# Attention plus top-2 expert layer on one core: second expert matmul in split float16, experts ordered by block count, weights converted piece by piece during the blocks, weight norms on TensorE

## The chip, the cores and the metric

The kernel runs on one core of a Trainium2 chip. The metric is device time in microseconds (us) of one execution. A core has TensorE (PE; its weight loads are listed as PEld), VectorE (DVE), ScalarE (ACT), GpSimd (POOL) and SyncE (SP), which here only issues transfers. Each has its own instruction stream; they meet at semaphores. In the profile an engine's name with a q (DVEq) is its instruction sequencer, which loads registers, waits for semaphores and hands work to the engine proper.

## What is computed

Input x is 16 tiles of 128 tokens with 256 features. First a channel attention with a residual, then an expert layer with a residual:

```
x   = x + xattn(layernorm(x), ctx, ctx)          # 4 heads, attention over channels, two weight sets
xf  = layernorm(x)                               # 2048 tokens x 256
logits = xf @ gate_w                             # 8 experts
top_w, top_idx = top_k(logits, 2);  combine = softmax(top_w) scattered
h   = gelu(xf @ w1[e] + b1[e])                   # 256 -> 1024
y   = h @ w2[e] + b2[e]                          # 1024 -> 256
out = x + sum_e combine[t, e] * y[e]
```

## The kernel before

**Attention stage.** 16 tiles pass through a software pipeline of 24 iterations (`attention(i, u)`, one function per engine, i from -4 to 19; iterations 4 to 9 are a loop, the rest is unrolled). In iteration i, PE forms the channel scores of tile i+1 (L913), transposes the context of tile i+2 (L921), transposes the normed output of tile i-3 (L929), multiplies with the values for tile i-1 (L937), forms the router logits of tile i-4 (L948), and last transposes the probabilities of tile i (L956), which wait for DVE (L726). DVE normalizes and scales (L660, L670, L713, L726) and adds the residual (L734, tile i-1). POOL makes k (L473, L476) and the inverse deviations (L461, L464).

**First-layer weights.** w1 (8 MB) lands in the storage of `W2`. ACT squares it (L570) in iterations 4 to 11, a ones-matmul sums the squares (L902), POOL takes the power -0.5 (L486), and each expert is scaled and split into a float16 high and low part in `W1`. Six experts are split inside iterations 13 to 19 by ACT (L575, L580), DVE (L697, L702) and POOL (L491); the last two after the stage, by ACT (L600, L604) and POOL (L500). Only when an expert is split can w2 of that expert be loaded over it (L375, L381).

**Routing.** DVE picks the two best experts of each token (L783 to L794, twelve small dependent operations), PE counts ranks, DVE gives each expert's tokens slots padded to blocks of 128 (L799 to L822), builds one-hot tables (L827, eight times), and the table of experts per block (L845 to L850). PE turns the one-hots into a list of rows per slot (L973), which becomes `row_of` (L854).

**Blocks.** There are NB = 39 blocks of 128 token slots, in order of the expert's number. `experts(i, u)` is one iteration on each engine:

```
PE:   transpose rows of block i+1 (L985); first layer of block i, 48 float16 matmuls (L999:
      high*high, high*low, low*high); second layer of block i-1, 8 float32 matmuls of 256 columns
      that the profile shows as 16 records (L1010); bias from three bfloat16 parts (L1012)
ACT:  high part of the rows of block i+1 (L622); Gelu of block i in two halves (L628)
DVE:  low part of block i+1 (L865); read the expert's number of block i+1 (L868) and take its
      routing weight (L870); read the number of block i (L873); hidden = psum*scale + b1 of
      block i in two halves (L877); output of block i-1 times routing weight (L887)
POOL: gather rows of block i+2 (L520, L526); scatter-add block i-2 to DRAM (L532, L537)
SP:   copy the split first-layer weights of block b into XW, two buffers (L393)
```

The hidden activations hT and the second-layer weights are float32. The order on every engine is as written. The sequencer of an engine stops at a semaphore wait, and every `value_load` is a TENSOR_LOAD and register work on it. After the last block the sums are read back and written out (L407, L637).

## Time and profile before

| | |
|---|---|
| median of 3 runs (lowest, highest) | 463.03 us (462.89, 463.79) |
| span of the profiled execution, first to last instruction | 460.8 us |
| the profiled execution's own time | not listed apart; the runs are 2.1 to 3.0 us above its span |
| busy: PE, DVE, ACT, POOL | 360.7, 238.7, 159.8, 234.3 us |
| attention and conversions / routing / blocks / write-back | 0 to 139 / 139 to 171 / 171 to 439 / 439 to 461 us |

A group row reads: line, engine, operation, output<-input by the program's names, shapes, count; then busy time and mean of one in ns; then the idle time of the engine just before, and what ended it. A row of the timeline reads: start in us, us, engine, line, operation, and in brackets the idle time before it and who ended it. A line of the chain reads: start, us, what the execution waited for. Profiled starts are from the start of the span.

### The profile page before, as it was taken

How to read it: one execution, taken by the hardware profiler on the slowest of the kernel's cores; microseconds unless marked ns; L12 is line 12 of the kernel's file. 1: busy time of each engine (PE TensorE's matmuls, PEld its weight loads, DVE VectorE, ACT ScalarE, POOL GpSimd, SP SyncE). 2: the span in 40 equal slices, each digit the busy share in tenths (PEclk: the TensorE clock that was granted, in tenths of full speed). 3: DMA queues.
4: the chain of work that ended last, by engine and by line, in shares of the span. 5: the costliest groups of instructions: out<-in, count | busy, mean ns of one | idle time of the engine just before them, and what ended most of it. 6: DMA issues, size and time to landing. Idle time of an engine off the chain costs nothing.

```text
span 460.8 us, 10869 instructions
## 1 busy us (share of the span) xinstructions
PE 360.7 (78%) x3229; PEld 315.9 (69%) x3230; DVE 238.7 (52%) x457; ACT 159.8 (35%) x399; POOL 234.3 (51%) x286
## 2 busy tenths in 40 slices
PE   0366778898630139999999999999999999999910
PEld 0356777797530028888988988888898898888800
DVE  1899988999899943433433333343343333334200
ACT  1335888867657003122212212222221221222100
POOL 6778777796879223434444543544444454352220
PEclk9999555555555558999999999999999999999965
DMA  7897665521279546566567557556656755764148
GB/s 132 254 317 216 183 175 146 161 69 45 65 243 346 158 155 230 165 225 197 155 220 219 157 195 228 174 171 226 202 153 215 222 158 191 228 181 153 22 84 303
DMA packets 55430, 84.54 MB, mean 183 GB/s; under 512 B 22578, under 2 KB 46996, under 8 KB 50420
## 3 DMA queue, kind: packets, MB, share of 16 engines
q1 hardware_dynamic: 43444, 71.24, 43.5%
q0 software_dynamic: 7680, 10.91, 14.9%
q10 hardware_dynamic: 4288, 2.18, 1.5%
q8 instruction: 8, 0.13, 0.1%
q14 instruction: 10, 0.08, 0.1%
HBM read 31.67 MB, written 11.74 MB: 94 GB/s over the span
## 4 chain that ended last, share of the span: by engine, by line
PE 56%; DMA 1%; issue 1%; POOLq 0%; POOL 0%; DVE 0%; DVEq 0%; ACT 0%
PE bank L1010 29%; PE bank L999 22%; PE bank L985 3%; PE bank L1012 2%; DMA shared<-xn_rows,gix 1%; POOLq L71 0%; POOL acc_rows L537 0%; DVEq L868 0%; DVE shared L887 0%; DVE shared L865 0%; ACT shared L622 0%; POOL six L532 0%; DVE w_of L870 0%; POOLq L536 0%; POOLq L537 0%
## 5 line engine op out<-in xcount | busy, mean ns | idle before, releaser
L1010 PE MATMUL bank<-W,shared 128*128 x624 | 143.3, 383 | 0.0
L1010 PEld LDWEIGHTS bank<-W,shared 128*128 128x128 f32 x624 | 115.5, 190 | 14.2
L999 PE MATMUL bank<-shared,X 128*128 128x128 f16 x1872 | 112.1, 220 | 0.5 <-issue 0.5
L537 POOL DMA_INDIRECT acc_rows<-shared,six x39 | 62.6, 1604 | 98.0 <-DVE shared L887 87.6
L999 PEld LDWEIGHTS bank<-shared,X 128*128 128x128 f16 x1872 | 108.9, 99 | 1.3 <-issue 0.7
L628 ACT ACTIVATE shared<-shared 128x512 f32<-128x512 f32 x78 | 49.1, 630 | 114.4 <-DVE shared L877 113.3
L887 DVE TENSOR_SCALAR shared<-bank,w_of 128x256 f32<-128x256 f32 x39 | 18.9, 484 | 106.7 <-PE bank L1012 106.7
L877 DVE SCALAR_TENSOR_TENSOR shared<-bank,h_unscale,b1T 128x512 f32<-128x512 f32 x78 | 55.3, 747 | 34.5 <-PE bank L999 20.8
L526 POOL DMA_INDIRECT shared<-xn_rows,gix x39 | 39.5, 1012 | 38.7 <-POOL gix L520 29.8
L622 ACT ACTIVATE shared<-bank 128x256 f16<-128x256 f32 x39 | 15.0, 384 | 102.3 <-PE bank L985 102.3
L520 POOL COPY gix<-row_of 128x1 int32 (+1 forms) x39 | 26.6, 683 | 7.4 <-DVE row_of L854 7.4
L937 PEld LDWEIGHTS bank<-shared 128*128 128x128 f32 x128 | 28.5, 326 | 1.8 <-ACT shared L557 1.8
L937 PE MATMUL bank<-shared 128*128 128x64 f32 x128 | 28.5, 402 | 1.0 <-ACT shared L557 0.9
L473 POOL TENSOR_TENSOR shared<-CX,shared 128x512 f32<-128x512 f32 x16 | 23.7, 1481 | 7.1 <-DMA CX<-in_ctx 7.1
L592 ACT ACTIVATE shared<-bank,vcols 128x128 f32<-128x128 f32 x64 | 24.1, 462 | 4.1 <-PE bank L937 3.5
L956 PE MATMUL bank<-ident,shared 128*128 128x128 f32 x32 | 10.5, 428 | 18.6 <-DVE shared L726 18.6
L865 DVE SCALAR_TENSOR_TENSOR shared<-bank,shared 128x256 f16<-128x256 f32 x39 | 16.6, 425 | 14.5 <-ACT shared L622 14.4
L476 POOL TENSOR_TENSOR shared<-shared 128x512 f32<-128x512 f32 x16 | 22.6, 1415 | 1.3
L563 ACT ACTIVATE shared<-bank,nmax 128x64 f32<-128x64 f32 x64 | 19.3, 318 | 11.0 <-DVE nmax L647 11.0
L985 PE MATMUL bank<-ident,shared 128*128 128x128 f32 x78 | 17.6, 308 | 6.5 <-DMA shared<-xn_rows,gix 6.5
L913 PEld LDWEIGHTS bank<-shared 128*64 128x64 f32 x256 | 14.4, 212 | 10.4 <-issue 10.4
L913 PE MATMUL bank<-shared 128*64 128x64 f32 x256 | 17.3, 311 | 5.5 <-POOL shared L476 4.0
(136 smaller groups left out, 426.7 us busy)
## 6 DMA issues: line engine op xcount, KB each, us to landing
X<-W SPq DMA_DIRECT2D x39, 1024.0 KB, 5.0
W<-in_L_ffn_w SPq DMA_DIRECT2D x16, 512.0 KB, 4.3
W<-in_L_ffn_w SPq DMA_DIRECT2D x8, 1024.0 KB, 6.6
CX<-in_ctx SPq DMA_DIRECT2D x32, 128.0 KB, 2.9
X<-in_x SPq DMA_DIRECT2D x4, 512.0 KB, 5.5
acc_rows<-X SPq DMA_DIRECT2D x16, 128.0 KB, 2.3
xn_rows<-xn SPq DMA_DIRECT2D x16, 128.0 KB, 2.2
X<-acc_rows SPq DMA_DIRECT2D x8, 256.0 KB, 5.2
```

The lines of the kernel that those rows point to most:

```text
L473: pool.tensor_tensor(k[:, n].rearrange("p g (h e) -> p g h e", e=HD), c, KW.rearrange("p g (h e) -> p g h e", e=HD), ALU.mult).then_inc(km ...
L520: pool.tensor_copy(gix[:, n:n + 1], row_of[:, bass.ds(b, 1)]).then_inc(gix_ok, 1)
L526: pool.indirect_dma_start(out=XG[:, n, :], out_offset=None, in_=xn_dram, in_offset=bass.IndirectOffsetOnAxis(ap=gix[:, n:n + 1], axis=0))\
L537: pool.indirect_dma_start(out=acc_dram, out_offset=bass.IndirectOffsetOnAxis(ap=six[:, n:n + 1], axis=0), in_=Y[:, n, :], in_offset=None, ...
L592: act.activation(vT[:, n, h, :], pCT[n][:, h, :], ACT.Identity, bias=vcols[:, NH + h:NH + h + 1], scale=vcols[:, h:h + 1]).then_inc(vt_ok, 1)
L628: act.activation(hT[:, n, 4 * m:4 * m + 4, :], hb[:, 4 * m:4 * m + 4, :], ACT.Gelu)\
L877: dve.scalar_tensor_tensor(out=hb[:, 4 * m:4 * m + 4, :], in0=pHT[n][m], scalar=h_unscale[:, bass.ds(e, 1)], in1=b1T[:, bass.ds(e * FC + 4 ...
L913: mm = pe.matmul(pS[n][h * HD:(h + 1) * HD, c, g, :], q[:, n, g, ch], k[:, n, g, ch], start=True, stop=True)
L937: mm = pe.matmul(pO[:, h * HD:(h + 1) * HD], vT[:, n, h, :], aT[:, h // 2, (h % 2) * HD:(h % 2 + 1) * HD], start=True, stop=True)
L985: mm = pe.transpose(pGT[:, c, :], XG[:, n, c * P:(c + 1) * P], ident[:, :])
L999: mm = pe.matmul(pHT[n][m][:, f % 4, :], XW[:, n, c, w, f * P:(f + 1) * P], XT[:, n, x, c, :], start=(c == 0 and w == 0 and x == 0), stop= ...
L1010: pe.matmul(pY[n], hT[:, n, f, :], W2[:, bass.ds(e, 1), f, :].rearrange("p a d -> p (a d)"), start=(f == 0), stop=False)
```

## The change

1. **Second layer in split float16.** w2 is scaled and split into high and low like w1, and so is the hidden activation. The 8 float32 matmuls of a block become 24 float16 matmuls of 256 columns. ACT writes Gelu to `hf` (float32) and then, after its own result, the scaled high part `hT[.., 0]`; DVE writes the low part `hT[.., 1]`. The unscaling goes into the routing weight and b2.
2. **Weights stay where they land** (`W`, nine slots) and are converted in 32 pieces of 1024 columns, one per block: the high part on ACT, the low part on DVE. Each converted expert goes to the slot of the expert before it, the first to a spare slot. Pieces 0 to 3 are made before and in iteration -1; iteration i of the block loop makes piece i+4, for i from 0 to 27. Iterations 28 to 40 convert nothing.
3. **Experts are ordered by block count**, most first, so that the expert of rank r cannot begin before block 4r. DVE computes ranks, the permutation and two tables per block (expert, slot).
4. **Weight norms on TensorE.** All 16 weight halves (w1, w2 of 8 experts, 1 MB each) are loaded during the attention stage, one per iteration from -4. In iterations 1 to 16 PE multiplies each half's top 16 bits, read as bfloat16, with itself: 16 matmuls of 128 columns into one bank. DVE takes the diagonals every fourth iteration (`traces`). ACT's squares and all conversions of the attention stage and behind it are gone.
5. The context transposes have one bank in place of two and come after the logits; b1 is transposed ahead of the attention stage on PE and ACT; b2's three small transfers are issued by ACT after its iteration 2; all 24 attention iterations are unrolled; blocks loop by four. SP does not copy first-layer weights for blocks 0 to 3; PE reads them in the spare slot.

```diff
@@ PE, end of an attention iteration (new)
+                w = i - GRAM
+                if 0 <= w < 2 * E:
+                    pe.wait_ge(w_in[w % 4], 16 * (w // 4 + 1))
+                    after(pe, trace_ok, w // 4)
+                    for j in range(2 * PIECE // P):
+                        x = (w // E) * 2 * PIECE + j * P
+                        cols = Wtop[:, w % E, x:x + P, 1:2].rearrange("p x o -> p (x o)")
+                        mm = pe.matmul(pGram[:, w % 4, :], cols, cols, start=(j == 0), stop=(j == 2 * PIECE // P - 1))
+                    mm.then_inc(gram_ok, 1)
@@ DVE
+            def traces(r):
+                dve.wait_ge(gram_ok, 4 * (r + 1))
+                dve.tensor_tensor(gsq, pGram, ident[:, :].rearrange("p (o f) -> p o f", o=1).broadcast_to([P, 4, P]),
+                                  ALU.mult).then_inc(diag_ok, 1)
+                dve.wait_ge(diag_ok, r + 1)
+                dve.tensor_reduce(wsq[:, 4 * r:4 * r + 4], gsq, AX.X, ALU.add).then_inc(trace_ok, 1)
...
@@ conversions taken out of ACT's and DVE's attention and of POOL's (the late ones also)
-                        act.activation(squares, W1in[:, bass.ds(e, 1), c, :].rearrange("p a f -> p (a f)"), ACT.Square,
-                                       accum_out=w1sq[:, bass.ds(e, 1), c]).then_inc(sq_ok, 1)
...
-                    act.activation(W1[:, e, 0, 0, :], W1in[:, e, 0, :], ACT.Copy, scale=w1scale[:, e:e + 1])\
-                       .then_inc(high_ok[0], 1)
...
-                    dve.scalar_tensor_tensor(out=W1[:, e, 0, 1, :], in0=W1in[:, e, 0, :], scalar=w1scale[:, e:e + 1],
-                                             in1=W1[:, e, 0, 0, :], op0=ALU.mult, op1=ALU.subtract).then_inc(low_ok[0], 1)
...
-                    pool.tensor_tensor(W1[:, e, c, 1, :], W1in[:, e, c, :], W1[:, e, c, 0, :], ALU.subtract)\
-                        .then_inc(low_late, 1)
@@ ACT, block iteration i
+                if not isinstance(i, int) or 0 <= i < CONVERTED - 4:
+                    if u == 0:
+                        held["dst"] = act.value_load(perm[0:1, bass.ds(g + 1, 1)], min_val=0, max_val=E)
+                        held["src"] = act.value_load(perm[0:1, bass.ds(g + 2, 1)], min_val=0, max_val=E - 1)
+                    act.wait_ge(low_ok, i + 1)
+                    high(u, bass.ds(held["src"], 1), bass.ds(held["dst"], 1), wscale[:, u // 2, bass.ds(held["src"], 1)])
                     for m in range(2):
                         act.wait_ge(hb_ok, 2 * b + (m + 1))
-                        act.activation(hT[:, n, 4 * m:4 * m + 4, :], hb[:, 4 * m:4 * m + 4, :], ACT.Gelu)\
-                           .then_inc(gelu_ok, 1)
+                        after(act, lo_ok, 2 * b + (m - 1))
+                        act.activation(hf[:, part, :], hb[:, part, :], ACT.Gelu).then_inc(gelu_ok, 1)
+                        act.wait_ge(gelu_ok, 2 * b + (m + 1))
+                        act.activation(hT[:, n, 0, part, :], hf[:, part, :], ACT.Copy, scale=hscale[:, bass.ds(e, 1)])\
+                           .then_inc(hi_ok, 1)
@@ DVE, iteration -1 of the blocks
+                if isinstance(i, int) and i == -1:
+                    for k in range(2, 4):
+                        dve.wait_ge(high_ok, k + 1)
+                        low(k, first, spare_slot, wscale[:, 1, first])
+                    dve.tensor_tensor(y_scale[:, :], wscale[:, 1, :], hscale[:, :], ALU.mult).then_inc(b2_scaled, 1)
...
+                    dve.tensor_tensor(B2[:, :, :], B2[:, :, :], y_scale[0:3, :].rearrange("r (e o) -> r e o", o=1)
+                                      .broadcast_to([3, E, D]), ALU.mult).then_inc(b2_scaled, 1)
@@ DVE, block iteration i
+                if converting and u == 0:
+                    held["dst"] = dve.value_load(perm[0:1, bass.ds(g + 1, 1)], min_val=0, max_val=E)
+                    held["src"] = dve.value_load(perm[0:1, bass.ds(g + 2, 1)], min_val=0, max_val=E - 1)
                     for m in range(2):
                         dve.wait_ge(h_ok, 2 * b + (m + 1))
+                        dve.scalar_tensor_tensor(out=hb[:, part, :], in0=pHT[n][m],
                                                  scalar=h_unscale[:, bass.ds(e, 1)],
...
+                        if m == 0 and converting:
+                            dve.wait_ge(high_ok, i + 5)
+                            low(u, bass.ds(held["src"], 1), bass.ds(held["dst"], 1),
+                                wscale[:, u // 2, bass.ds(held["src"], 1)])
+                    for m in range(2):
+                        dve.wait_ge(hi_ok, 2 * b + (m + 1))
+                        dve.scalar_tensor_tensor(out=hT[:, n, 1, part, :], in0=hf[:, part, :],
+                                                 scalar=hscale[:, bass.ds(e, 1)], in1=hT[:, n, 0, part, :],
+                                                 op0=ALU.mult, op1=ALU.subtract).then_inc(lo_ok, 1)
@@ PE, second layer of block b = i-1
-                    pe.wait_ge(gelu_ok, 2 * (b + 1))
                     for f in range(FC):
-                        pe.matmul(pY[n], hT[:, n, f, :], W2[:, bass.ds(e, 1), f, :].rearrange("p a d -> p (a d)"),
-                                  start=(f == 0), stop=False)
+                        if f % 4 == 0:
+                            pe.wait_ge(lo_ok, 2 * b + (f // 4 + 1))
+                        for w, h in ((0, 0), (0, 1), (1, 0)):
+                            x = (2 * (2 + f // 4) + w) * PIECE + (f % 4) * D
+                            pe.matmul(pY[n], hT[:, n, h, f, :], whole(Wh[:, slot, x:x + D]),
+                                      start=(f == 0 and w == 0 and h == 0), stop=False)
```

**DVE in the blocks.** One iteration of the loop. Before, from the read of the expert's number (expert) to the output (w_of is the routing weight):

```order
L873 TENSOR_LOAD expert
L873 ISA x2
L875 REGISTER_ALU
L32 REGISTER_ALU [waits h_ok]
L877 ISA [waits gelu_ok]
L877 SCALAR_TENSOR_TENSOR shared<-bank,h_unscale,b1T 128x512
L875 REGISTER_ALU
L877 ISA [waits gelu_ok,h_ok]
L877 SCALAR_TENSOR_TENSOR shared<-bank,h_unscale,b1T 128x512
L32 REGISTER_ALU [waits y_ok]
L887 REGISTER_ALU [waits got_w,added]
L887 TENSOR_SCALAR shared<-bank,w_of 128x256
```

With the change, in the same place, from the first half of the hidden layer to the second low part (L926 is a weight piece's low part, L980 the activation's):

```order
L968 SCALAR_TENSOR_TENSOR shared<-bank,h_unscale,b1T 128x512
L974 REGISTER_ALU
L926 ISA [waits high_ok]
L926 ISA
L926 SCALAR_TENSOR_TENSOR W<-W,wscale 128x1024
L966 REGISTER_ALU
L968 ISA [waits gelu_ok,h_ok]
L968 SCALAR_TENSOR_TENSOR shared<-bank,h_unscale,b1T 128x512
L980 REGISTER_ALU [waits hi_ok]
L980 SCALAR_TENSOR_TENSOR shared<-shared,hscale 128x512
L980 SCALAR_TENSOR_TENSOR shared<-shared,hscale 128x512 [waits hi_ok]
```

A piece of 1024 columns stands between the two halves, and two operations that wait for ACT stand ahead of the output, where there were none.

**PE in the attention stage.** One iteration before (the context transposes are L921, the probabilities' transposes L956):

```order
L913 MATMUL bank<-shared 64x64 [waits exp_ok,k_ok,q_ok]
L913 MATMUL bank<-shared 64x64 x7
L921 MATMUL bank<-ident,CX 128x128 [waits vt_ok,c_in1]
L921 MATMUL bank<-ident,CX 128x128 x3
L929 MATMUL bank<-ident,xn 128x128 [waits xn_ok]
L929 MATMUL bank<-ident,xn 128x128
L937 MATMUL bank<-shared 128x64 [waits x1_ok,vt_ok,as_ok]
L937 MATMUL bank<-shared 128x64 x3
L956 MATMUL bank<-ident,shared 128x128 [waits as_ok,pr_ok]
L956 MATMUL bank<-ident,shared 128x128
```

With the change, the second half of one iteration and the start of the next (L1028 values, L1038 logits, L1046 context, L1054 probabilities, L1066 a weight half with itself, L1012 scores):

```order
L1028 MATMUL bank<-shared 128x64 [waits x1_ok,vt_ok,as_ok]
L1028 MATMUL bank<-shared 128x64 x3
L1038 MATMUL bank<-GW,W 128x8 [waits xts_ok]
L1038 MATMUL bank<-GW,W 128x8
L1046 MATMUL bank<-ident,W 128x128 [waits vt_ok,c_in1]
L1046 MATMUL bank<-ident,W 128x128 x3
L1054 MATMUL bank<-ident,shared 128x128 [waits as_ok,pr_ok]
L1054 MATMUL bank<-ident,shared 128x128
L1066 MATMUL bank<-W 128x128 [waits trace_ok,w_in0]
L1066 MATMUL bank<-W 128x128 x15
L1012 MATMUL bank<-shared 64x64 [waits exp_ok,k_ok,q_ok]
```

Sixteen matmuls stand between the probabilities' transposes and the next scores.

## Rows read from the trace of the kernel before

**Rows 1.** The page's 40 slices (11.5 us each): TensorE's busy tenths and granted clock
```profile
PE   0366778898630139999999999999999999999910
PEclk9999555555555558999999999999999999999965
```

**Rows 2.** The chain that ended last, one block of 39
```profile
185.01 0.37 PE bank L985 x2
185.38 2.68 PE bank L999 x48
188.06 3.51 PE bank L1010 x16
191.57 0.21 PE bank L1012
```

**Rows 3.** Timeline of one block: DVE, ACT and POOL's scatter
```profile
253.02 0.48 DVE L887 TENSOR_SCALAR shared<-bank,w_of 128x256 f32<-128x256 f32 x1 [2.62 <-PE bank L1012]
253.18 0.38 ACT L622 ACTIVATE shared<-bank 128x256 f16<-128x256 f32 x1 [2.12 <-PE bank L985]
253.70 0.42 DVE L865 SCALAR_TENSOR_TENSOR shared<-bank,shared 128x256 f16<-128x256 f32 x1 [0.19 <-ACT shared L622]
...
254.42 1.61 POOL L537 DMA_INDIRECT acc_rows<-shared,six  x1 [2.58 <-DVE shared L887]
254.57 0.15 DVE L870 COPY w_of<-shared  x1 [0.45 <-issue]
...
255.54 1.41 DVE L877 SCALAR_TENSOR_TENSOR shared<-bank,h_unscale,b1T 128x512 f32<-128x512 f32 x2 [0.81 <-issue]
...
256.32 1.29 ACT L628 ACTIVATE shared<-shared 128x512 f32<-128x512 f32 x2 [2.76 <-DVE shared L877]
```

**Rows 4.** Line L868 in 252.5 to 256 us: DVE's sequencer reads an expert's number
```profile
L868 DVEq TENSOR_LOAD <-expert x1: 304/304/304, 253.8 to 253.8; - x1
```

**Rows 5.** Lines L702, L575: low and high part of 1024 columns (ns min/median/max)
```profile
L702 DVE SCALAR_TENSOR_TENSOR W<-W,w1scale x6: 1273/1274/1277, 112.4 to 138.1; 128x1024 f16<-128x1024 f32 x6
L575 ACT ACTIVATE W<-W,w1scale x6: 1138/1144/1222, 108.2 to 130.5; 128x1024 f16<-128x1024 f32 x6
```

**Rows 6.** Timeline of one attention iteration, PE and DVE
```profile
83.86 0.69 PE L956 MATMUL bank<-ident,shared 128*128 128x128 f32 x2 [0.50 <-DVE shared L726]
...
84.48 1.12 PE L913 MATMUL bank<-shared 128*64 128x64 f32 x16
...
90.48 0.69 PE L956 MATMUL bank<-ident,shared 128*128 128x128 f32 x2 [1.04 <-DVE shared L726]
```

**Rows 7.** Line L734, the residual add of the 16 tiles
```profile
L734 DVE TENSOR_TENSOR X<-bank,X x16: 409/412/418, 32.8 to 128.6; 128x256 f32<-128x256 f32 x10, 128x256 f32 x6
```

**Rows 8.** Timeline from the first routing operation to the mask
```profile
139.32 0.28 DVE L783 TENSOR_REDUCE m<-bank 128x16 f32<-128x128 f32 x1
...
141.39 8.52 POOL L500 TENSOR_TENSOR W<-W 128x1024 f16<-128x1024 f32 x4
...
145.83 2.10 DVE L785 TENSOR_TENSOR shared<-shared,iotaE 128x128 f32<-128x128 f32 x1
...
150.09 0.69 DVE L794 TENSOR_TENSOR chosen<-shared 128x128 bf16<-128x128 f32 x1
```

**Rows 9.** Timeline of later routing operations: a small one, one of 312 columns
```profile
152.14 0.17 DVE L805 TENSOR_TENSOR_SCAN cslot<-onesE,cnt_blk 128x8 f32<-128x8 f32 x1
...
160.35 0.48 DVE L845 TENSOR_TENSOR shared<-iotaB,cslot 128x312 f32<-128x312 f32 x1
```

**Rows 10.** Timeline of the first block: rows known, low part, first layer
```profile
166.19 0.20 DVE L854 SCALAR_TENSOR_TENSOR row_of<-bank,tv 128x39 int32<-128x39 f32 x1
...
171.87 0.43 DVE L865 SCALAR_TENSOR_TENSOR shared<-bank,shared 128x256 f16<-128x256 f32 x1 [5.48 <-ACT shared L622]
...
173.04 4.01 PE L999 MATMUL bank<-shared,X 128*128 128x128 f16 x48
```

**Rows 11.** Line L1012: the bias matmul that ends each block
```profile
L1012 PE MATMUL bank<-B,ones x39: 277/278/278, 184.7 to 438.8; 3*128 x39
```

478 lines of the change are left out of this document (279 added, 199 removed).

## The prediction

> **What bounds the kernel now.** I read the page's slices first, then the chain that ended last, then the timeline of one block, one attention iteration and the routing. The slices show two regimes [rows 1]: from 171 us on TensorE is busy all the time at the full clock (2.4 GHz); up to there it is busy 6 to 9 tenths at mostly half of it. In the blocks the chain is TensorE alone [rows 2]: 0.37 us of transposes, 2.68 of first layer, 3.51 of second layer, 0.21 of bias, 6.77 us for a block with no gap. DVE in the same block waits 2.62 us for TensorE and 0.19 for ACT, and the rest of its pauses end with "issue", which is its own sequencer [rows 3]. The last block's bias matmul starts at 438.8 us, the first one's at 184.7 [rows 11].
>
> In the attention stage the residual add of tile 0 is at 32.8 us and that of tile 15 at 128.6 [rows 7], so 6.39 us per tile. In the iteration shown TensorE waits 1.04 us of 6.62 for DVE's probabilities [rows 6]: it has 5.6 us of work at the low clock, and DVE sets the pace, with little in hand. Between tile 15 and the mask come 10.7 us to the first routing operation and 11.5 us for twelve dependent routing operations [rows 7, 8]. The operation on 128 columns takes 0.28 us in the first row and 2.10 in a later one, while POOL does the late conversions beside it [rows 8].
>
> **The blocks.** TensorE loses 3.51 us and gains 24 float16 matmuls of 256 columns. A float16 matmul of 128 columns takes 2.68/48 = 0.056 us [rows 2], so I take 0.110 for 256; half of one of the 16 float32 records, 3.51/16 = 0.219, is the same. 24 x 0.110 = 2.6 us, and a block by TensorE alone is 6.77 - 3.51 + 2.63 = 5.89 us. The Trainium skill ("TensorE: Matmul & The Clock Gate", section on the back-to-back issue gap) gives about 81 ns as the sustained pace of 128-column matmuls with their weight loads; the row's 56 ns is below it, so the row decides.
>
> The gain is not the 0.88 us per block, since DVE now has a cycle of its own that nothing of TensorE's opens: the second low part waits for ACT's second high part, that for the second Gelu, and that for DVE's second half of the hidden layer. I follow it from the issue of the second low part.
> - Output and low part of the next rows (L887, L865) follow. From one to the other took 0.68 us with 0.19 of waiting [rows 3], so 0.5. One after the other behind a low part of some 0.7 us this is 1.1 us, but the sequencer runs ahead while the engine works: it started the read of an expert's number at 253.8, when L865 ran until 254.1 [rows 3, 4]. So I take 0.5, and keep 1.1 as the other end.
> - From L865 to the first half of the hidden layer 255.54 - 253.70 = 1.84 us pass, two reads of the expert's number with their register work [rows 3]. They stay.
> - First half 0.66 us to the next (1.41 for two, less 0.75), the weight piece 1.2 (1.27 with its end) [rows 3, 5].
> - Second half 0.75, Gelu 0.63, high part 0.63 (1.29 for two Gelus [rows 3]; the copy of 1024 columns takes 1.14 [rows 5]), and 0.2 for three handovers: 2.2 us. The first low part fits in this wait.
> - Two more reads in one iteration of four (L960, L961) and the branch: 2 x 0.75/4 + 0.05 = 0.43 us.
>
> Sum 0.5 + 1.84 + 0.66 + 1.2 + 2.2 + 0.43 = 6.83 us in the 28 converting iterations, 7.4 with the other end. ACT's work in it is 0.38 + 1.14 + 4 x 0.63 = 4.0 us and hides. Without the piece and the extra reads DVE's cycle is 5.2 us, so TensorE's 5.89 holds for the last ones. From the end of block 0's second layer to that of block 38's: 27 x 6.83 = 184.4, 9 x 5.89 = 53.0, and 5.5 and 3.0 for the last two, which have no transposes or no first layer: 245.9 against 438.8 - 184.7 = 254.1 us [rows 11]. **Blocks: -8.2 us.**
>
> **First block.** The first bias matmul is 18.5 us behind the table of rows (184.7 - 166.2 [rows 10, 11]). Now DVE does L865 at +5.5 as before [rows 10], the read and weight 0.9, two pieces 2.4, then b2's scaling, 2048 columns on three partitions; no row has it, and it lies between one piece's 1.2 and twice it; I take 2.2, by its columns. With the reads that queue behind it the hidden layer starts at +12.7; 0.66 + 1.2 + 2.2 + 0.75 and half a second layer later (1.4) the block is through: +19.0. **First block: +0.5 us.** Pieces 0 and 1 hide in the 5.5 us of waiting for the gather.
>
> **Routing.** Gone is the conversion work. After tile 15 a diagonal step (two operations of 512 columns at 0.75 [rows 3], 1.5 us) comes ahead of the norm, but the operations that POOL held up shrink: I count 7.1 us to the first routing operation instead of 10.7. The twelve operations take 0.3 each, 4.1 us instead of 11.5 [rows 8]. **-11.0 us**; DVE's conversions there are not moved to another place on this path. Added are six more small operations for ranks and permutation and five for scales, at 0.17 to 0.3 each [rows 9], +2.6; and for the block tables sixteen operations instead of three, six of them on 312 columns at 0.45 each [rows 9], 3.9 us instead of 1.1, +2.8. All are chained on DVE. **+5.4 us.**
>
> **Attention.** 16 matmuls of 128 columns come on TensorE in 16 iterations. The 48 of the first block took 4.01 us and began at the low clock [rows 10], 48 at the full clock 2.68 [rows 2]; so 0.107 each low, 0.056 full, 1.7 or 0.9 us per iteration. At the low clock TensorE then has 5.6 + 1.7 = 7.3 us against DVE's 6.39 and becomes the bound. At the full clock it has less than DVE, which has 6.39 plus four diagonal steps of 1.5 us over 16 tiles: 6.7. The clock was mostly low at 85% busy [rows 1, 6]; at 100% it rose in the first block [rows 10], so I expect it to change to and fro: 6.9, **+8 us** over 16 iterations; ends +5 and +14. At the start TensorE and ACT wait for b1's rows, the context of tile 2 is queued behind 2 MB of weights, and ACT issues three transfers: +3; ends +1 and +6. The last tiles lose conversions: -0.7. **Attention: +10.3 us.** ACT's squares cost nothing before, since ACT was not the bound; taking them away gives nothing.
>
> **Sum.** 10.3 - 11.0 + 5.4 + 0.5 - 8.2 = -3.0 us on a span of 460.8, which gives 457.8. The runs are 2.1 to 3.0 us above the span; from the median of 463.03 it is **460.0 us**.
>
> **Rivals.**
> - **DVE's cycle costs more** (slower). If output, low part and reads add up in series, a converting block takes 7.4 us or more, 27 x 0.6 = +16: **476 us**. For it: two pauses of 0.45 and 0.81 us by "issue" in one block [rows 3]. Against: the read that began under L865 [rows 4]. It decides from 6.95 us per converting block on, where the sum passes 463.
> - **TensorE at the low clock through the attention stage** (slower): 7.3 us for each of 16 tiles, +14.6 instead of +8: **467 us**. For it: the low clock at 85% busy.
> - **DVE and POOL get in each other's way** (slower). The low parts of weights and activations each read two operands in SBUF, three operations per block, while POOL works 3.5 us per block on gathers and scatters. If each such operation waits 0.3 us, 28 x 0.9 = +25: **485 us**. For it: 0.28 us becoming 2.10 beside POOL [rows 8]. Against: the routing weight's copy at 254.57 was not held up by the scatter that ran on POOL from 254.42 to 256.03 [rows 3]. The Trainium skill ("SBUF — State Buffer", Who interferes with whom) has it as a rule: a DVE instruction with two SBUF inputs contends with a GpSimd instruction that reads SBUF. By that rule these three, and not L877 or L865 with one operand in PSUM, are exposed; what POOL's indirect transfers read no row shows.
> - **DVE does not bind** (faster): if its reads vanish in ACT's wait, TensorE's 5.89 us holds for all blocks, 27 x 0.94 = -25: **435 us**.
> - **Attention is not slowed** (faster): the added matmuls lie in TensorE's waits and lift the clock, +2 instead of +10.3: **452 us**.
>
> **Chances.** Forecast case 0.45 (452 to 467 by its own bounds); DVE's cycle 0.18; low clock 0.12; POOL 0.07; DVE not binding 0.10; attention not slowed 0.08. The range 447 to 480 leaves out DVE not binding and POOL, and little of the others: about 2 in 10. 0.2%, 0.9 us, is about what a measurement of this kernel can tell from no change. The forecast case is faster in 0.28 of its 0.45, the same in 0.06 and slower in 0.11; with the rivals: faster 0.46, same 0.06, slower 0.48. It is close to even; the two signs come from terms of 8 to 11 us that nearly cancel.
>
> **What would show it.** Right: outputs (L988) 6.8 us apart up to block 27, then 5.9; TensorE waiting for DVE's low part L980 in the first part and for nothing later; residual adds 6.9 us apart in the attention stage; twelve routing operations of 0.3 us. Wrong: outputs 5.9 us apart from the start, or over 7.2; low parts of the activation taking well over 0.75 us; the mask later than it was; the granted clock low in a block.

## The result, and the profile after

The changed kernel takes 487.2 us (median of 5 runs, 483.77 to 493.39), the one before on the same chip 462.89: a ratio of 1.049, 95% interval 1.046 to 1.053. It is **slower by 24 us**, where 460 was predicted and 480 was the end of the range. Medians are of all runs of a kernel, while the ratios and intervals, here and below, leave out the runs more than 1.5% above its fastest, as the profiled one is: it took 492.72 us, 5.5 more than the median, with a span of 490.9. So the differences by stage add up to 30 us and not to 24:

| stage, by its marks in the trace | before | after | difference | predicted |
|---|---|---|---|---|
| start to the residual add of tile 0 | 32.8 | 36.1 | +3.3 | +3 |
| tile 0 to tile 15 | 95.8 | 110.5 | +14.7 | +7.3 |
| tile 15 to the mask | 21.5 | 8.7 | -12.8 | -11.0 |
| mask to the table of rows | 16.1 | 22.3 | +6.2 | +5.4 |
| table of rows to the first bias matmul | 18.5 | 19.3 | +0.8 | +0.5 |
| first to last bias matmul | 254.1 | 270.4 | +16.3 | -8.2 |
| last bias matmul to the end | 22.0 | 23.6 | +1.6 | 0 |

The marks are these rows, each line's own over the whole run (where a line has a count, minimum, median and maximum in ns, then first and last start), and they answer to [rows 7, 8, 10, 11]:

```profile
L729 DVE TENSOR_TENSOR X<-bank,X x16: 415/424/425, 36.1 to 146.6; 128x256 f32<-128x256 f32 x16
L920 DVE SCALAR_TENSOR_TENSOR row_of<-bank,tv x1: 199/199/199, 177.6 to 177.6; 128x39 int32<-128x39 f32 x1
L1138 PE MATMUL bank<-B,ones x39: 277/278/278, 196.9 to 467.3; 3*128 x39
```

The timeline of the routing shows the part that went as forecast, twelve operations of 0.3 us with nothing between them, against [rows 8]:

```profile
151.71 0.29 DVE L779 TENSOR_REDUCE m<-bank 128x16 f32<-128x128 f32 x1 [2.08 <-issue]
152.04 0.29 DVE L780 TENSOR_TENSOR shared<-bank,m 128x128 f32<-128x128 f32 x1
152.36 0.29 DVE L781 TENSOR_TENSOR shared<-shared,iotaE 128x128 f32<-128x128 f32 x1
...
155.27 0.69 DVE L790 TENSOR_TENSOR chosen<-shared 128x128 bf16<-128x128 f32 x1
```

So two stages failed, attention by 7 us and the blocks by 24 (in this execution). The page's rows of TensorE, against [rows 1], and its costliest group and the context transposes:

```profile
PE   0337676868682038978778788787987889889900
PEclk9999867665887557999999999998999999999965
...
L1118 PE MATMUL bank<-shared,X 128*128 128x128 f16 x1680 | 101.3, 221 | 40.5 <-issue 24.6
...
L1046 PE MATMUL bank<-ident,W 128*128 128x128 f32 x64 | 16.2, 402 | 33.6 <-ACT shared L574 27.4
```

In the blocks TensorE, busy 9 tenths and more before, is at 7 to 8, at full clock, and loses 40.5 us ahead of the first layer, 24.6 of them by its own issue. In attention it idles 27.4 us until ACT's copies (L574) of the transposed context of the tile before.

**A block without conversion**, from TensorE's timeline. It should have taken 5.89 us and takes 6.8:

```profile
428.97 2.78 PE L1136 MATMUL bank<-W,shared 128*128 x24
431.69 0.28 PE L1138 MATMUL bank<-B,ones 3*128 x1
431.89 0.44 PE L1094 MATMUL bank<-ident,shared 128*128 128x128 f32 x2
433.11 2.84 PE L1118 MATMUL bank<-shared,X 128*128 128x128 f16 x48 [0.77 <-issue]
```

The matmuls are as forecast (2.7 us for the 24). What is new is 0.77 us by issue between transposes and first layer. There TensorE's sequencer reads two numbers from SBUF, the on-chip memory that the engines share: the expert (L1098) and, new, the weight slot (L1102). From 230 to 430 us the slot's read takes up to 1.15 us, not the 0.3 of [rows 4]:

```profile
L1102 PEldq TENSOR_LOAD <-wslot x27: 300/817/1153, 234.4 to 424.7; - x27
```

**A block with conversion**, DVE's timeline:

```profile
267.36 0.75 DVE L980 SCALAR_TENSOR_TENSOR shared<-shared,hscale 128x512 f16<-128x512 f32 x1 [0.87 <-ACT shared L632]
268.03 0.48 DVE L988 TENSOR_SCALAR shared<-bank,w_of 128x256 f32<-128x256 f32 x1
268.42 0.41 DVE L941 SCALAR_TENSOR_TENSOR shared<-bank,shared 128x256 f16<-128x256 f32 x1
268.75 0.15 DVE L946 TENSOR_TENSOR w_of<-shared,y_unscale  x1
269.66 0.75 DVE L968 SCALAR_TENSOR_TENSOR shared<-bank,h_unscale,b1T 128x512 f32<-128x512 f32 x1 [0.76 <-issue]
270.32 1.28 DVE L926 SCALAR_TENSOR_TENSOR W<-W,wscale  x1
271.52 0.75 DVE L968 SCALAR_TENSOR_TENSOR shared<-bank,h_unscale,b1T 128x512 f32<-128x512 f32 x1
272.19 0.75 DVE L980 SCALAR_TENSOR_TENSOR shared<-shared,hscale 128x512 f16<-128x512 f32 x1
273.81 0.75 DVE L980 SCALAR_TENSOR_TENSOR shared<-shared,hscale 128x512 f16<-128x512 f32 x1 [0.87 <-ACT shared L632]
```

From one second low part to the next 6.45 us pass: in this block the sum of the prediction is there (6.4 without the reads of the permutation). Two of its pieces are not, and cancel: from the second low part to L941 it is 1.06 us and not 0.5, and from there to L968 1.24 and not 1.84. DVE's two reads happened to be short (0.32 and 0.30 us). The outputs (L988) of the 24 blocks 4 to 27 are 7.24 us apart on average, 7.1, 6.8, 6.6 and, in the first step of each four, 8.4; those of blocks 28 to 36 are 6.84 apart.

**An attention iteration**, PE's and then ACT's timeline (L1066 are the products, L1012 the scores, L1028 the output, L1038 the router logits):

```profile
78.19 1.91 PE L1066 MATMUL bank<-W 128*128 128x128 bf16 x16
80.03 1.12 PE L1012 MATMUL bank<-shared 128*64 128x64 f32 x16
...
82.20 0.56 PE L1038 MATMUL bank<-GW,W 128*128 128x8 f32 x4
84.78 1.08 PE L1046 MATMUL bank<-ident,W 128*128 128x128 f32 x4 [2.02 <-ACT shared L574]
...
86.09 1.91 PE L1066 MATMUL bank<-W 128*128 128x128 bf16 x16
```

```profile
82.86 0.38 ACT L568 ACTIVATE W<-bank 128x256 f32<-128x256 f32 x1 [2.86 <-PE bank L1038]
83.14 1.50 ACT L574 ACTIVATE shared<-bank,vcols 128x128 f32<-128x128 f32 x4
```

This is a ring: products, scores, rows' transposes, output and logits on TensorE; then ACT, released by the logits' matmuls (the rows' copy has one buffer, which they read), copies the rows and the context; then the context transposes, which write the single bank that ACT has just read (a bank is one of the eight parts of PSUM, the memory into which TensorE writes); then the probabilities' transposes and the products again. Nothing in it overlaps. DVE, which set the pace before, is busy 68.0 of 111 us between 36 and 147 us (before: 87.4 of 96).

### The profile page after: what moved, and what is told of

It reads as the page before. It is cut to its first block, busy times and chain, and to the rows that moved or that the text cites. A ratio compares the mean times of both kernels' runs of the same rounds, so it can differ in the third digit from the quotient of the medians.

```text
span 490.9 us, 12813 instructions
## 1 busy us (share of the span) xinstructions
PE 341.1 (69%) x3795; PEld 298.7 (61%) x3796; DVE 294.5 (60%) x590; ACT 208.2 (42%) x458; POOL 234.5 (48%) x275
## 3 DMA queue, kind: packets, MB, share of 16 engines
q1 hardware_dynamic: 42740, 67.04, 40.5%
## 4 chain that ended last, share of the span: by engine, by line
PE 22%; issue 11%; DVE 10%; DVEq 8%; ACT 6%; DMA 2%; ACTq 0%; POOLq 0%; POOL 0%
PE bank L1118 11%; PE bank L1136 9%; DVE W L926 5%; DVE shared L968 3%; ACT shared L629 3%; ACT shared L632 2%; DVEq L963 2%; DVEq L944 2%; PE bank L1094 1%; DVE shared L988 1%; DMA acc_rows<-shared,six 1%; DMA shared<-xn_rows,gix 1%; PE bank L1138 1%; DVEq L961 1%; DVEq L968 1%
## 5 line engine op out<-in xcount | busy, mean ns | idle before, releaser
L1118 PE MATMUL bank<-shared,X 128*128 128x128 f16 x1680 | 101.3, 221 | 40.5 <-issue 24.6
L1136 PE MATMUL bank<-W,shared 128*128 (+1 forms) x936 | 109.4, 273 | 0.8 <-DVE shared L980 0.6
L536 POOL DMA_INDIRECT acc_rows<-shared,six x39 | 62.5, 1604 | 83.9 <-DVE shared L988 74.6
L1136 PEld LDWEIGHTS bank<-W,shared 128*128 128x128 f16 x936 | 89.1, 98 | 12.6 <-issue 2.0
L968 DVE SCALAR_TENSOR_TENSOR shared<-bank,h_unscale,b1T 128x512 f32<-128x512 f32 x78 | 58.4, 749 | 52.1 <-PE bank L1118 27.5
L980 DVE SCALAR_TENSOR_TENSOR shared<-shared,hscale 128x512 f16<-128x512 f32 x78 | 58.6, 751 | 35.9 <-ACT shared L632 35.9
L632 ACT ACTIVATE shared<-shared,hscale 128x512 f16<-128x512 f32 x78 | 56.3, 722 | 13.0 <-ACT shared L629 8.0
L591 ACT ACTIVATE W<-W,wscale (+1 forms) x32 | 36.2, 1140 | 15.0 <-issue 7.7
L519 POOL COPY gix<-row_of 128x1 int32 (+1 forms) x39 | 37.1, 951 | 10.2 <-DVE row_of L920 10.1
L926 DVE SCALAR_TENSOR_TENSOR W<-W,wscale (+1 forms) x32 | 40.7, 1276 | 1.0 <-issue 0.9
L1046 PE MATMUL bank<-ident,W 128*128 128x128 f32 x64 | 16.2, 402 | 33.6 <-ACT shared L574 27.4
L1046 PEld LDWEIGHTS bank<-ident,W 128*128 128x128 f32 x64 | 10.6, 202 | 35.1 <-issue 28.6
L485 POOL TENSOR_TENSOR shared<-W,shared 128x512 f32<-128x512 f32 x16 | 23.3, 1456 | 13.2 <-DMA W<-in_ctx 13.2
L531 POOL COPY six<-row_of 128x1 int32 (+1 forms) x39 | 16.1, 412 | 27.1 <-DMA acc_rows<-shared,six 27.0
L1066 PE MATMUL bank<-W 128*128 128x128 bf16 x256 | 28.0, 291 | 0.0
L574 ACT ACTIVATE shared<-bank,vcols 128x128 f32<-128x128 f32 x64 | 24.1, 464 | 7.2 <-PE bank L1028 6.4
L1066 PEld LDWEIGHTS bank<-W 128*128 128x128 bf16 x256 | 26.2, 137 | 0.8
```

The lines of the kernel that those rows point to most:

```text
L519: pool.tensor_copy(gix[:, n:n + 1], row_of[:, bass.ds(b, 1)]).then_inc(gix_ok, 1)
L536: pool.indirect_dma_start(out=acc_dram, out_offset=bass.IndirectOffsetOnAxis(ap=six[:, n:n + 1], axis=0), in_=Y[:, n, :], in_offset=None, ...
L591: act.activation(whole(piece(dst, k, 0)), whole(piece(src, k)), ACT.Copy, scale=scales).then_inc(high_ok, 1)
L632: act.activation(hT[:, n, 0, part, :], hf[:, part, :], ACT.Copy, scale=hscale[:, bass.ds(e, 1)])\
L926: dve.scalar_tensor_tensor(out=whole(piece(dst, k, 1)), in0=whole(piece(src, k)), scalar=scales, in1=whole(piece(dst, k, 0)), op0=ALU.mult ...
L968: dve.scalar_tensor_tensor(out=hb[:, part, :], in0=pHT[n][m], scalar=h_unscale[:, bass.ds(e, 1)], in1=b1T[:, bass.ds(e * FC + 4 * m, 4)] . ...
```

## The experiments

Two theories to start with. For the blocks: the reads of numbers on TensorE and DVE cost more than the prediction gave them. Rivals: DVE's operations are the bound; the gathers are. For attention: the single bank, and the place of the diagonals, cost more than the products. Rival: the products' own time. The gathers can be struck off from the trace already: ahead of the transposes of the gathered rows (L1094) TensorE has no idle time from 230 to 390 us.

One caution comes first. Five of the kernels below change attention only and have the change's code in the blocks; from first to last bias matmul their profiles have 265.1 to 269.1 us, and the change's has 270.4. Differences of 5 us there say nothing. Attention scatters too: over the seven kernels with products and one bank the residual add of tile 15 stands at 144.3 to 146.6 us, over the five with products and two banks at 124.9 to 129.5. Each place below is from one profile.

### TensorE's read of the expert moved into the second layer

```diff
-                    e = pe.value_load(expert[0:1, bass.ds(b, 1)], ...)      # ahead of the first layer
                     for f in range(FC):
+                        if f == 4:
+                            e = pe.value_load(expert[0:1, bass.ds(b, 1)], ...)
```

> The changed kernel with one edit: TensorE's sequencer reads the expert's number (for the bias matmul alone) in the middle of the second layer instead of beside the read of the weight slot ahead of the first layer. Theory (TensorE's two reads cost the idle 0.77 us by issue ahead of the first layer, and are the bound of the last ten blocks): outputs of the non-converting blocks 6.0 us apart instead of 6.9, so -8 us there; the converting blocks with one read less on DVE's path (u not 0) go from about 6.9 to DVE's own cycle of 6.45, -5 to -9 us; first blocks unchanged. Total 470 to 476 us against 487. Rival (the pause is the wait for the gathered rows or for the slot's DMA, and issue only its name): no change within 2 us. Rival (DVE binds all converting blocks): only the non-converting blocks gain, -8 us.

486.18 us, ratio 1.052 (1.044 to 1.059): nothing gained. But the last blocks did go from 6.84 to 5.94 us, as the theory had it; the converting ones stood at 7.46 instead of 7.24. The second rival held there: from 230 to 390 us TensorE now waits 13.4 us for DVE's low part ahead of the second layer (L1137), where it waited for nothing (L1136). Its -8 us did not come, since the converting blocks gave back what the others gained.

### One read less on DVE

```diff
-                    e = dve.value_load(expert[0:1, bass.ds(b, 1)], ...)
+                    e = e_now if u > 0 and block_on(b + 1) else dve.value_load(expert[0:1, bass.ds(b, 1)], ...)
```

> The changed kernel with one edit: DVE keeps the expert's number that it read for block b+1 and uses it again for block b in the next step, except at the start of each four; 27 of 37 steps have one read less on DVE. Theory (the steps without the reads of the permutation are bound by TensorE with its two reads, only the first of each four by DVE): the outputs of the first step of each four stay 8.4 to 9.1 us apart, the others stay at 6.4 to 7.4, together -2 to -5 us. Rival (DVE's cycle binds in all converting blocks): 21 converting steps lose 0.7 us each, -15 us, outputs 6.0 to 6.2 us apart there. Rival (the reads are hidden in waits for TensorE): no change.

486.57 us, ratio 1.051 (1.047 to 1.055). The steps are 6.4, 6.9, 7.5 and 8.0 us apart, the blocks 262.7 us: at most 2.4 us below the band. Alone it does nearly nothing, as the theory had it.

### Both

> The two edits of the first two runs together: TensorE reads the expert's number in the middle of the second layer, and DVE uses the number read for the next block again in the next step. Theory (in the steps without reads of the permutation TensorE and DVE each have a cycle near 6.5 to 6.9 us, so that one edit alone lays bare the other): together more than the sum of 3.4 and 7.7 us that each took out of the blocks: those steps at 5.9 to 6.2 us, the first step of each four still 8.4; from the first to the last bias matmul 250 to 256 us against 270.4. Rival (the edits simply add): 258 to 260. Rival (the same wait twice): 262.

472.54 us, ratio 1.023 (1.015 to 1.031); the blocks 254.1 us. Together the edits are worth 14.7 us of the median, apart 1.0 and 0.6, which is within the scatter. TensorE's and DVE's cycles lay close to each other and each covered the other's gain. The steps came to 6.0, 6.5, 6.8 and 8.2, not all to 5.9: the read of the slot was still ahead of the first layer, with 0.77 us by issue.

### DVE's read where it waits for ACT

```diff
                     for m in range(2):                       # the two low parts of the activation
+                        if m == 1 and block_on(i + 1):
+                            held["e"] = dve.value_load(expert[0:1, bass.ds(i + 1, 1)], ...)
                         dve.wait_ge(hi_ok, 2 * b + (m + 1))
```

The weight of the next block's rows moves to the step's end.

> TensorE's read split as before, and on DVE the number for block b+1 is read where DVE waits for the second high part anyway (0.87 us, twice seen in each block), the weight of the next block's rows following at the step's end; only the first step of each four reads the number again, beside the two of the permutation. Theory (reads cost only where nothing covers them): steps without reads of the permutation at TensorE's own 5.9 to 6.1 us, the first of each four at 8.0; from the first to the last bias matmul 240 to 250 us; total 452 to 464. Rival (the read delays the second low part as much as it did elsewhere): 256 us or more, like the run with one read. Rival (the late weight holds back the next gather): TensorE waits for the gathered rows.

472.27 us, ratio 1.020 (1.014 to 1.026): the blocks fell by 4.6 us to 249.5, but the total missed its 452 to 464, since the first bias matmul now stands 22.8 us behind the table of rows (19.4 in the run before). That is the last rival, the late weight, which is taken up at the end. DVE now waits for TensorE in each step shown (0.41 to 2.11 us by L1124), and its wait for ACT is 0.87 us as before: the read is free there. TensorE binds, with the slot's read, and its two reads tell something. Lines L1108 (slot, behind the transposes) and L1139 (expert, in the middle of the second layer), 230 to 430 us:

```profile
L1108 PEldq TENSOR_LOAD <-wslot x30: 795/930/991, 231.0 to 425.8; - x30
...
L1139 PEldq TENSOR_LOAD <-expert x30: 297/302/312, 235.6 to 430.0; - x30
```

The same instruction on the same engine takes 0.93 us in one place and 0.30 in the other. In the trace of the changed kernel I sorted the reads of all engines by the time since SP last issued the copy of a block's first-layer weights (1 MB within SBUF): 54 reads in its first microsecond, mean 0.30 us (32 of them SP's own); 36 in the second, 0.92 (TensorE's 26 and DVE's 10 alike: 0.92 and 0.90); 20 in the third, 0.86; 39 in the fourth, 0.59; 63 later, by microseconds 0.29 to 0.32. The kernel before has the same copy. There 74 of DVE's 78 reads up to 430 us stand in the fifth microsecond or later and take 0.31 us; two in the second took 1.03 and two in the fourth 0.60. The read of [rows 4] was one of the 74.

### The copy made small

```diff
-                sp.dma_start(XW[:, u % 2], Wh[:, bass.ds(s, 1), 0:4 * PIECE]...).then_inc(w1s_in[u % 2], 16)
+                sp.dma_start(XW[:, u % 2, 0, 0:1, 0:128], Wh[:, bass.ds(s, 1), 0:128]).then_inc(w1s_in[u % 2], 16)
```

The kernel leaves out the right first-layer weights from block 4 on; its instructions and waits stay.

> The changed kernel with the copy of each block's first-layer weights cut from 1 MB to 32 KB (both staging buffers are filled once before; from block 4 on the first layer uses the wrong weights, so the computation is left out in that sense; all instructions and waits stay). Theory (a read of a register takes 0.3 us, and 0.9 us while the 1 MB copy inside SBUF is in flight, as the trace of the changed kernel shows by the time since the copy's start: 0.30 us in its first microsecond and from the fifth on, 0.92 in the second): all reads 0.27 to 0.35 us, TensorE's pause ahead of the first layer falls from 0.77 to 0.2 or less in the last ten blocks (6.2 us or less apart instead of 6.9), the first to the last bias matmul 250 to 258 us against 270. Rival (the long reads come from something that stands in the same place, POOL's gathers or the engines' own pipelines): reads of 0.9 us remain, blocks within 3 us of 270.

472.02 us, ratio 1.021 (1.019 to 1.023); blocks 248.8 us, 16 us below the band of 265 to 269. The same slot read as L1102 above is line L1107 here:

```profile
L1107 PEldq TENSOR_LOAD <-wslot x30: 294/301/308, 231.8 to 425.4; - x30
```

TensorE's timeline of a late block, without a pause, 5.88 us from bias to bias:

```profile
414.08 0.28 PE L1143 MATMUL bank<-B,ones 3*128 x1
414.29 0.44 PE L1099 MATMUL bank<-ident,shared 128*128 128x128 f32 x2
414.56 2.84 PE L1123 MATMUL bank<-shared,X 128*128 128x128 f16 x48
417.24 2.78 PE L1141 MATMUL bank<-W,shared 128*128 x24
419.96 0.28 PE L1143 MATMUL bank<-B,ones 3*128 x1
```

The theory holds: the long reads are the copy's doing. With short reads the converting blocks take 6.89 us (6.6, 6.4, 6.5, 8.0) and the others 5.79. **The prediction had 6.83 and 5.89.** Its sums were right for reads of 0.3 us, for the converting blocks with the two pieces that cancel.

### TensorE's slot read moved too, in a row or apart

> As the run with the reads in DVE's gap, and TensorE also reads the weight slot one block ahead, in the middle of the second layer, except at the start of each four. Theory (the slot's read behind the second layer costs 0.7 us of idle time on TensorE in each step, and DVE's cycle of 5.1 us lies below TensorE's 5.9): steps without reads of the permutation at 5.9 to 6.2 us instead of 6.7, the last blocks at 5.9 instead of 6.2, the first of each four unchanged at 7.4; from the first to the last bias matmul 236 to 242 us instead of 249.5; total 459 to 465. Rival (both reads in a row in the middle of the second layer drain TensorE's queue just as well): 247 or more. Rival (something else, the gather or the transfer of the slot, holds the steps at 6.7): no change.

469.92 us, ratio 1.017 (1.015 to 1.018); blocks 245.5 us. The steps are 6.1, 6.5, 6.5 and 7.6, the last 6.2; the blocks lose 4.0 us more, where 7.5 to 13.5 were expected, since two reads in a row cost 0.45 to 0.60 us by issue in the middle of the second layer, less than the 0.7 they replaced. Partly the first rival.

> All edits together as before, and TensorE's two reads of the second layer stand apart, one after its sixth and one after its fifteenth matmul, instead of in a row after the twelfth. Theory (one read of some 0.75 us with its register work is hidden by the matmuls queued ahead, two in a row are not: 0.45 to 0.60 us of idle time by issue in the middle of the second layer): that idle time goes, the steps without permutation reads are 5.9 to 6.1 us instead of 6.5, the last blocks 5.8 instead of 6.2; from the first to the last bias matmul 231 to 236 us instead of 245.9; total 10 to 14 us less than the run before. Rival (DVE's cycle of about 5.9 to 6.4 us with the read in its gap comes next): 240 to 243. Rival (a read behind only six matmuls meets the slot's copy in flight): pauses move, no change.

462.18 us, ratio 0.993 (0.988 to 0.997), with the shared bank of below in it as well, and so to be held against that run's 454.26: **slower by 8 us**, blocks 254.7 us instead of 245.9. The last rival had the reason, a read that meets the copy, but not that it costs. The second read now starts 1.6 us behind the first, in the middle of the copy (0.96 us instead of 0.30), and has only the nine matmuls since the first read queued ahead of it:

```profile
309.23 1.87 PE L1152 MATMUL bank<-W,shared 128*128 x15
312.19 1.15 PE L1152 MATMUL bank<-W,shared 128*128 x9 [1.09 <-issue]
```

### The permutation's reads between the low parts

> As the run with the reads apart, and in the first step of each four DVE's two reads of the permutation and the low part of the weight piece stand between the two low parts of the activation, where DVE waits for ACT. Theory (the first step of each four is longer because of these reads): 6.3 to 6.8 us instead of 7.9 (with its two halves added), 7 x 1.2 = -8 us in the blocks. Rival (the second low part then comes later and TensorE waits for it): no change or +3 us. Rival (the reads meet the slot's copy and take 0.9 us each, and ACT's own reads in that step come after them): -3 us.

477.9 us, ratio 1.031 (1.025 to 1.036); blocks 269.3 us, to be held against the 254.7 of the run with the reads apart. Wrong: the first rival, and far beyond its 3 us. The steps became 5.6, 9.3, 6.5 and 9.1; with the piece between them the second low part is late, and TensorE's second layer with it.

### Attention without the products

The products and their diagonals on DVE are left out, and the norms a constant. "Products" below means both.

> The changed kernel without the products of the weights with themselves on TensorE and their diagonals on DVE: the norms of both weight matrices are a constant, so the computation leaves the norms out; all else, the single bank for the transposed context too, stays. Theory (the longer attention stage comes from TensorE's wait for the single bank and from the diagonals standing in DVE's order, not from the time of the added matmuls): residual add of tile 15 at 134 to 138 us instead of 146.6: the peaks of 9.9 us in every fourth iteration go, the others stay at 7.0 to 7.5. Rival (the added matmuls are the whole cost): tile 15 at 132 or below, 6.4 us per tile as before the change. Rival (single bank is all): tile 15 at 144 or later.

Tile 15 at 132.8 us (before 128.6, after 146.6): no peaks. Most steps are 7.0 us. The theory's 134 to 138 was not low enough; the products cost 13.8 us here, and the wait for the bank is still there, 26.1 us:

```profile
L1048 PE MATMUL bank<-ident,W 128*128 128x128 f32 x64 | 15.8, 394 | 31.9 <-ACT shared L575 26.1
```

> As the run without the products (norms of the weight matrices left out, a constant in their place), and with the second bank for the transposed context given back, as in the kernel before. Theory: tile 15 at 129 to 132 us, 6.4 us per tile or less, and TensorE's idle time ahead of the context transposes falls from 33 us to under 8; the difference to the run with one bank, 4 to 8 us, is the price of the bank. Rival (the bank costs nothing, since another wait takes its place): within 1.5 us of the run with one bank.

Tile 15 at 120.7 us, most steps 6.1, and that wait is gone. The bank alone is worth 12.1 us:

```profile
L1048 PE MATMUL bank<-ident,W 128*128 128x128 f32 x64 | 17.5, 429 | 6.4 <-DMA W<-in_ctx 6.4
```

### The diagonals later in the iteration

```diff
-                    traces(r)        # at the iteration's head
...
+                    traces(r)        # behind the scaling of the probabilities
```

> The changed kernel with one edit: DVE's diagonal step stands behind the scaling of the probabilities in its iteration instead of at the iteration's head, where it waits for the products that TensorE issues last in the iteration before. Theory (the peaks of 9.9 us in every fourth attention iteration are that wait and the step's 1.5 us in series): the peaks fall to 8.0 to 8.8, residual add of tile 15 3 to 6 us earlier than 146.6 (141 to 144). Rival (the peak is only the step's own time plus the products): within 1.5 us of 146.6. Rival (behind the probabilities it delays the residual add, which TensorE waits for): later than 147.

Tile 15 at 145.8 us, total 486.95 us (ratio 1.050, 1.042 to 1.057). The peaks of 9.9 fell to 8.2 to 8.9, and their neighbours grew: the first rival, within the scatter of 144.3 to 146.6. In this ring it did not matter where the step stood.

### Two banks for the context, with the products

```diff
-        pCT = [ps[n][:, :].rearrange("p (h n) -> p h n", h=NH) for n in (2, 2)]
+        pCT = [ps[n][:, :].rearrange("p (h n) -> p h n", h=NH) for n in (2, 5)]
-        pXT = ps[5][:, 0:D].rearrange("p (c n) -> p c n", c=C)
+        pXT = ps[3][:, D:2 * D].rearrange("p (c n) -> p c n", c=C)      # beside pAT, used in turn
-                    after(pe, vt_ok, 4 * t)
+                    after(pe, vt_ok, 4 * (t - 1))
```

PE's rows' transposes move behind the output's matmuls and wait for ACT's copy of the probabilities.

> The changed kernel with the transposed probabilities and the transposed normalized rows in one bank of PSUM (two halves, used in turn) so that the transposed context has two banks again; products and diagonals stay. Theory (one bank for the context is worth about 12 us, as between the two runs without products, 132.8 and 120.7): residual add of tile 15 at 133 to 138 us instead of 146.6, total about 475 to 478. Rival (sharing puts a new wait in place of the old one): tile 15 within 3 us of 146.6. Rival (with the products the bank matters less, since TensorE has work of its own to put there): 139 to 143.

471.7 us, ratio 1.019 (1.013 to 1.024); tile 15 at 128.5 us, better than the theory's 133 to 138, and where the kernel before had it. TensorE's timeline shows the ring open, the context transposes L1047 straight behind the logits' matmuls:

```profile
74.94 0.69 PE L1012 MATMUL bank<-shared 128*64 128x64 f32 x16
75.56 1.10 PE L1021 MATMUL bank<-shared 128*128 128x64 f32 x8
76.50 0.39 PE L1030 MATMUL bank<-ident,W 128*128 128x128 f32 x2
76.72 0.51 PE L1039 MATMUL bank<-GW,W 128*128 128x8 f32 x4
77.09 0.63 PE L1047 MATMUL bank<-ident,W 128*128 128x128 f32 x4
79.22 0.44 PE L1056 MATMUL bank<-ident,shared 128*128 128x128 f32 x2 [1.50 <-DVE shared L721]
```

> The changed kernel without the products and diagonals (norms left out, a constant in their place) and with the bank shared as in the run of the shared bank. Theory (sharing costs nothing of its own; the products and diagonals cost the 8 us between 120.7 and 128.5): residual add of tile 15 at 120 to 122 us. Rival (sharing costs part of it): 124 to 127.

Tile 15 at 121.6 us, so in these two profiles sharing costs at most 0.9 us of its own. The four cases:

| residual add of tile 15 | no products | products |
|---|---|---|
| two banks | 120.7 (shared: 121.6) | 128.5 (shared) |
| one bank | 132.8 | 146.6 |

Products cost 6.9 us with two banks and 13.8 with one; the bank costs 12.1 without and 18.1 with them. By the scatter of these places 6.9 can be 3 to 8, and 18.1 can be 15 to 22. Each costs more beside the other. Even in the ring the products are not paid in full: on TensorE they are 28.0 us of work (L1066).

The table shows a gain as well. With two banks and without products tile 0 to tile 15 takes 85.6 us, where the kernel before takes 95.8; 7.5 of these 10.2 us are in the last five tiles, where that kernel converted weights.

A warning on the clock. From 36 to 115 us the profile with tile 15 at 120.7 us shows the low clock (0.50), the one with 121.6 us the full clock. TensorE's context transposes take the same in both (40 to 115 us, mean in ns behind the comma):

```profile
L1048 PE MATMUL bank<-ident,W 128*128 128x128 f32 x46 | 12.6, 428 | 0.0
...
L1049 PE MATMUL bank<-ident,W 128*128 128x128 f32 x45 | 12.4, 428 | 0.0
```

So TensorE was no faster in the second, whatever the clock shown. The changed kernel has the same ahead of its first shown change, at 50 us: its 16 products at 39 and 47 us take 1.91 us under a shown full clock, as they do later at a shown 0.50, where they take 1.08 at a shown 1.00 (135 and 138 us). The time of the matmuls is the safer sign.

### All that helped, together

The reads as in the run that gave 469.92 us, and the shared bank.

> The run before with the shared bank of PSUM too (all edits together; it computes the whole reference). Theory (the two stages are independent): tile 15 at 128 to 130 us and 16 us less than the run before, 441 to 450 us, faster than both kernels (462.6 and 487). Rival (attention's gain is given back in the first blocks, where the conversions wait for DMA or ACT): over 452.

454.26 us, faster than both kernels by the medians, by 8 us and by 33. All six runs (446.29 to 456.88) lie below all of the kernel before (461.77 to 463.04). The ratio, 0.968 (0.965 to 0.971), rests on the two lowest alone, 446.29 and 449.12; that of the medians is 0.982. The theory's 441 to 450 was not reached. Tile 15 at 129.5, blocks 245.9 us. The first bias matmul stands 22.9 us behind the table of rows, though, since POOL waits for the late weight before it gathers block 2's rows:

```profile
175.71 0.97 POOL L525 DMA_INDIRECT shared<-xn_rows,gix  x1 [7.12 <-DVE w_of L994]
```

> All edits together (TensorE's two reads in a row in the middle of the second layer, DVE's reads in the gap, the shared bank), and in the step ahead of block 0 alone the weight of its rows stands ahead of the pieces and of the second bias again. Theory (the weight behind the scaling of the second bias held back POOL's gather of block 2): from the table of rows to the first bias matmul 19 to 20 us instead of 22.9, the blocks as before, total 3 to 4 us less than the run of all edits: 444 to 451 us. Rival (the first hidden layer starts later by the same amount, since the read and weight come first on DVE): no change.

453.84 us, ratio 0.979 (0.975 to 0.982). The stage came down to 19.1 us as forecast, but the blocks had 250.5 us instead of 245.9. The two versions can't be told apart by their medians; that the total falls by 3 to 4 us was not shown.

## Why the prediction was wrong

- **Start, routing, first block: right.** +3.3 for +3; -12.8 for -11.0; +6.2 for +5.4; +0.8 for +0.5. The removed POOL work did give the routing's operations back their 0.3 us. Which of the three reasons made the start's +3 was not looked into, nor the tail's +1.6, which had no term. The table of the result has the first bias matmul on time, but the output of block 0 is 4.5 us behind it (0.3 before): on DVE it stands behind the low parts of block 1. No term had that.
- **Attention, +10.3: the step that failed is "At the low clock TensorE then has 5.6 + 1.7 = 7.3 us against DVE's 6.39 and becomes the bound".** It weighed busy times of two engines against each other. Neither bound: TensorE idled 27.4 us for ACT's copies, and DVE was busy 68.0 of 111 us. The change's one bank for the context transposes, which the description of the change and the diff had, was given no term at all; it closed a ring through TensorE and ACT, 12.1 us by itself and 18.1 with the products in it. The products with two banks cost 6.9 us, close to the +8 over 16 iterations.
- **A term of the other sign, "The last tiles lose conversions: -0.7" with "taking them away gives nothing", was mis-sized too:** 10.2 us are gained from tile 0 to tile 15 with two banks and no products. What of it is conversions, squares, the new order or the unrolling stays open. In these marks the stage is -10.2 for that, +7.4 for the products with two banks and +17.5 for the bank, together +14.7; the miss of only 7 us is luck.
- **The rival of the low clock: its number came, its reason did not.** It had +14.6 us for the stage, and +14.7 were measured. Its condition mostly held while the products ran: of their 16 groups the first eleven took 1.91 us each, the price at the low clock (the estimate was 1.7, from 0.107 per matmul; twice the full clock's 0.056 would give 1.8). But TensorE was not the bound, and with a second bank and the same products, 5 to 9 of the 16 groups at 1.8 us or more, the stage took 89.1 to 93.7 us. So the agreement is luck. The low clock does seem to cost something: in the two of these five profiles in which the last three groups took 1.08 to 1.09 us and not 1.87 to 1.91, tile 15 stands at 125 us and not at 128.5 to 129.5. What it costs inside the ring was not separated.
- **Blocks, -8.2: the term that was mis-sized is the reads, in "They stay" (1.84 us on DVE), "2 x 0.75/4" and the one left out, TensorE's second read.** They were taken from a read of 0.304 us [rows 4]. Beside the 1 MB copy a read takes 0.8 to 1.15 us, and the change put more reads there, above all TensorE's two (medians 0.90 and 0.75 us over the run; DVE's 0.31): outputs 7.27 us apart over the first 27 intervals for 6.83, and 6.84 over the next nine for 5.89. That is 11.9 and 8.5 us; some 4 us more are the first output, which stands 4.5 us behind the first bias matmul (0.3 before). With the copy made small the terms were right to 0.1 us (6.89, 5.79).
- **"TensorE alone 5.89" for the last blocks** had no term for a second read on TensorE's sequencer. The diff showed it.
- **The rival "DVE's cycle costs more", 476 us,** had the sign and the place, but not the reason: its 1.1 us for output and low part is there (1.06), but the stretch with the reads behind it is shorter by as much (1.24 for 1.84), and the block shown has 6.45 us.
- **DVE and POOL in each other's way: on DVE no, on POOL yes.** The low parts that read two SBUF operands take 0.751 and 1.276 us on average (L980, L926), 1.274 before [rows 5], with POOL at work in every block; the forecast 0.3 us per operation is not there. By the rule of the Trainium skill ("SBUF — State Buffer", Who interferes with whom) they and POOL's reads of SBUF would contend. POOL's side agrees: its copy of one column (L532 before, L531 after) took 0.18 us each time, and now takes up to 0.79 when such a low part is beside it (31 times, mean 0.47; the other eight 0.18 to 0.20). With the copy of the weights made small it is the same (mean 0.51). POOL does not bind the blocks: it waits 74.6 us for DVE's outputs ahead of its scatters (L536), so this costs nothing here. The two copies:

```profile
L532 POOL COPY six<-row_of x39: 182/183/193, 182.4 to 440.6; 128x1 int32 x34, 128x1 int32<-128x1 int32 x5
...
L531 POOL COPY six<-row_of x39: 182/336/789, 197.8 to 470.3; 128x1 int32 x34, 128x1 int32<-128x1 int32 x5
```

- **The pace of float16 matmuls** was right: 24 in 2.7 us.

## What to carry to other kernels

A number that a sequencer reads from SBUF is a step of its own on that engine: put it where the engine has a long queue or waits anyway, ahead of a large copy within SBUF or in its first microsecond, and check each place in the trace, since apart can be worse than in a row. A price read from one row holds for the place of that row. Before adding work to an engine "that has time", follow each buffer with a single copy around: if write, read and next write go through two engines in order, all that stands between is in series, and a bank given back can be worth more than the work. If two engines' cycles are within half a microsecond of each other, an edit to one alone measures as nothing; try both together before dropping either.
